# A ViT layer on one core: front's 64-row products widened to 128 rows with zero weights, its square roots taken off ScalarE, a head every 15 slots

## The chip, the cores and the metric

The kernel runs on one core of a Trainium2 chip, in one launch. The metric is the device time of that launch in microseconds (us), the median of three runs.

## The reference

64 images of 112x112 pass through one layer. All is float32; L = 65 tokens (a class token and 8x8), C = 64 channels, H = 8 heads of 8 channels.

```python
h = tok(x)                                 # two-level Haar maps, resized to 8x8, @ W + b: (64, 64, 64)
h = concat([cls_tok, h], axis=1)           # (64, 65, 64)
h = h + attn(layernorm(h))                 # cosine attention
h = h + ffn(layernorm(h))                  # product keys, top 16 of 4096 entries a head, then causal attention

# layernorm: (x - mean) / sqrt(var + 1e-5) over the 64 channels
# attn:      qn = q / max(norm(q), 1e-12), kn likewise, norms over the 8 channels of a head
#            softmax(qn @ kn.T * scale + bias) @ v for each head, then @ proj_w.T + proj_b
```

## The kernel before

**The main stream.** The images go through in ten passes (`PASSES`: 5, 7 seven times, 5, 5, with the two fives at the end; in all 64). A pass has t = 65 times its images as columns: 455 for seven, 325 for five. For each pass and each of the 8 heads the program streams a table of 32 chunks (`CH`) of 128 entries. A chunk is one **slot** `g`; there are 8 x 32 = 256 slots for a pass and 2,560 in all. In slot g TensorE spreads the scores of chunk g + 2 into one of three banks (`spread_scores`, L675, one float32r product of t + 1 columns), ScalarE takes the exponential of chunk g (`exp_unit`, L858), VectorE masks it (`mask_unit`, L1042), and TensorE adds the rows of chunk g - 1 (`add_rows`, L687, a float32 product, which is two instructions). The lead is three banks (`NA`) and four weight buffers (`RING`).

**Beside it.** In the same slots, after those four steps, each engine's program has work in a fixed place, counted modulo 32 (`u`, the chunk of the head): up to four tiles of token scores for the next head, one every 8 slots, with their top-16 search (`scores` L649, `best16` and `top24` on VectorE, `candidates`, `threshold` L443 to L453 and `low_parts` on GpSimd, `turn_scores` L658); and one `attend` for the head before (TensorE at u = 3, 6, 13, 16; VectorE at 4, 5, 9, 10, 17; GpSimd at 6 and 11).

**Front.** While pass p streams, `front` prepares pass p + 1: the maps, the first layernorm, q, k and v, the norms of q and k, eight attention tasks, the projection and the second layernorm. Its place is q, the slot modulo 256:

```python
MAPS, TOK, LN1 = ROWS + 3, ROWS + 6, ROWS + 10          # ROWS = 22, so LN1 = 32
QK, VAL, NRM, ATT = LN1 + 11, LN1 + 14, LN1 + 17, LN1 + 28
PERIOD = 16
```

A task starts at ATT + 16 j; in it TensorE works at steps 0, 8 and 11 (L585, L594, L603), VectorE at 1, 2, 6, 7 and 12, ScalarE at 5 and 9, GpSimd at -2 (`kx`, L412) and 3 (L418). A layernorm takes ten slots from its start (32, and six after the projection): product with `center` (L522), square (L766), copy (L913), one product an image with `mean` (L527), square root (L769), reciprocal (L916), transposes (L532), multiplication (L920). The norms of q and k are one product an image (L570), a square root on ScalarE (L800), a maximum and a reciprocal on VectorE (L936, L940), a spread over the channels on GpSimd (L403) and transposes (L577).

**Order and waits.** The order is written out: every engine loops over the same slots and queues what belongs to each, and then runs its queue strictly in order, waiting for semaphores. Nothing moves past a waiting instruction of its own engine. The front of pass 0 runs in slots -256 to -1, when no chunk streams, with tasks every four slots, beside the folding of the tables (64 groups: `fold`, L625, L822, L634, L991); this stretch is called the prologue here.

## Time and profile before

| | |
|---|---|
| median of three runs | 3162.47 us (3162.01 to 3162.71) |
| the profiled execution | 3162.24 us |
| its span in the trace | 3160.4 us |
| TensorE busy | 3085.8 us, 98% of the span |
| VectorE busy | 2437.1 us, 77% |
| ScalarE busy | 1809.5 us, 57% |
| GpSimd busy | 1102.9 us, 35% |
| prologue, up to the first chunk's spread | 134.6 us |

How to read it: DVE is VectorE, ACT ScalarE, POOL GpSimd, PE TensorE's products and PEld its weight loads, SP SyncE; L687 is line 687 of the kernel before. A matmul's end is modelled, and a group of products also counts as busy while one waits on the next load, so 98% doesn't say that TensorE is at its peak: the starts of successive spreads (L675) show the length of a slot.

### The profile page before, as it was taken

To read this page: it belongs to the slowest core of one execution; us is meant where nothing else is said; L and a number is where in the kernel's file an instruction comes from. 1 tells how busy PE (TensorE), PEld (TensorE's weight loads), DVE (VectorE), ACT (ScalarE), POOL (GpSimd) and SP (SyncE) were. 2 spreads that over 40 slices of the span, in tenths; PEclk is the share of its full clock that TensorE was granted. 3 is DMA by queue.
4 is the path that set the end of the run, shared out by engine and by line. 5 is a ranking of instruction groups with operands and counts; after the bars stand their busy time and mean duration, and the time that the engine had idled before them with its cause. 6 is when DMAs were issued, how large, how long until landed. Compare 5 with 4: busy or idle time off the path is not lost.

```text
span 3160.4 us, 56341 instructions
## 1 busy us (share of the span) xinstructions
PE 3085.8 (98%) x16588; PEld 2020.8 (64%) x16588; DVE 2437.1 (77%) x8690; ACT 1809.5 (57%) x4758; POOL 1102.9 (35%) x2712
## 2 busy tenths in 40 slices
PE   8999999999999999999999999999999999999998
PEld 8867656655666566656666666656655666676666
DVE  4678778877887788777877787778877887787776
ACT  4465565556555655556555655565556565655554
POOL 2234324433443334334433343334333433342331
PEclk9999999999999999999999999999999999999999
DMA  9110000011011101100001000100111001111110
GB/s 222 33 25 18 22 20 19 19 23 20 19 19 23 20 19 19 23 20 14 15 18 26 18 19 19 25 19 19 19 22 20 19 19 21 27 17 26 19 25 18
DMA packets 92763, 81.25 MB, mean 26 GB/s; under 512 B 56542, under 2 KB 87977, under 8 KB 92457
## 3 DMA queue, kind: packets, MB, share of 16 engines
q1 hardware_dynamic: 91505, 77.26, 11.9%
q8 instruction: 135, 2.21, 0.3%
q14 instruction: 171, 1.40, 0.2%
q10 hardware_dynamic: 952, 0.37, 0.1%
HBM read 38.77 MB, written 1.47 MB: 13 GB/s over the span
## 4 chain that ended last, share of the span: by engine, by line
PE 80%; DVE 8%; ACT 5%; issue 4%; POOL 3%; ACTq 0%; DMA 0%; POOLq 0%
PE ps L687 45%; PE ps L675 16%; DVE wts L1042 5%; ACT wts L858 3%; PE ps L716 2%; PE ps L649 2%; PE ps L700 2%; PE ps L603 2%; PE ps L585 2%; PE ps L634 2%; PE ps L658 2%; PE ps L594 1%; PE ps L705 1%; DVE top L1026 1%; PE ps L625 1%
## 5 line engine op out<-in xcount | busy, mean ns | idle before, releaser
L687 PE MATMUL ps<-wts,table 128*128 128x455 f32 (+1 forms) x5120 | 2200.5, 512 | 0.0
L1042 DVE SCALAR_TENSOR_TENSOR wts<-ps,wts 128x455 f32<-128x455 f32 (+1 forms) x2560 | 1473.6, 579 | 537.9 <-ACT wts L858 526.1
L675 PE MATMUL ps<-st,spread 128*128 128x456 f32 (+1 forms) x2560 | 1372.5, 536 | 51.8 <-DVE wts L1042 45.9
L858 ACT ACTIVATE wts<-ps 128x455 f32<-128x455 f32 (+1 forms) x2560 | 1219.3, 513 | 86.5 <-PE ps L675 83.4
L687 PEld LDWEIGHTS ps<-wts,table 128*128 128x128 f32 x5120 | 940.9, 190 | 190.1 <-issue 127.1
L675 PEld LDWEIGHTS ps<-st,spread 128*128 128x128 f32 x2560 | 483.5, 189 | 457.7 <-DVE wts L1042 326.9
L443 POOL TENSOR_SCALAR stat<-top 114x1 f32<-114x1 f32 (+1 forms) x296 | 79.4, 268 | 1317.1 <-DVE top L1026 1317.1
L829 ACT ACTIVATE sc<-ps 114x128 f32<-114x128 f32 (+1 forms) x296 | 82.2, 278 | 349.0 <-PE ps L649 349.0
L833 ACT ACTIVATE cand_e<-top,stat 114x16 f32<-114x16 f32 (+1 forms) x296 | 90.9, 307 | 311.5 <-POOL stat L450 311.2
L848 ACT ACTIVATE st<-ps 128x228 fp32r<-128x228 f32 (+1 forms) x296 | 106.6, 360 | 280.6 <-PE ps L658 280.6
L459 POOL TENSOR_TENSOR parts<-sc,parts 114x128 f32<-114x128 f32 (+1 forms) x296 | 135.3, 457 | 83.3 <-ACT parts L840 74.7
L473 POOL TENSOR_TENSOR s<-s,red 65x455 f32<-65x455 f32 (+1 forms) x80 | 70.6, 882 | 253.0 <-DVE red L1072 253.0
L658 PEld LDWEIGHTS ps<-ident,parts 114*128 114x128 f32 (+1 forms) x592 | 83.8, 142 | 112.2 <-issue 97.2
L1026 DVE MAX8 top<-cand_rest 114x8 f32<-114x100 f32 (+1 forms) x592 | 149.4, 252 | 0.0
L453 POOL TENSOR_SCALAR sc<-sc,stat 114x64 f32<-114x64 f32 (+1 forms) x296 | 138.1, 466 | 29.2
L427 POOL TENSOR_TENSOR cand<-best 114x64 f32<-114x64 f32 (+1 forms) x296 | 87.0, 294 | 135.0 <-DVE best L1010 134.7
L649 PEld LDWEIGHTS ps<-w_sim,xh 128*114 128x114 f32 (+1 forms) x444 | 78.5, 177 | 76.5 <-issue 66.6
L447 POOL TENSOR_SCALAR stat<-stat,top 114x1 f32<-114x1 f32 (+1 forms) x296 | 111.3, 376 | 32.8
L1008 DVE MATCH_REPLACE8 rest<-best,sc 114x64 f32<-114x64 f32 (+1 forms) x592 | 118.2, 205 | 0.0
L412 POOL TENSOR_SCALAR kx<-hx,head_of 64x455 f32<-64x455 f32 (+1 forms) x80 | 107.7, 1346 | 17.8 <-DVE hx L945 17.8
L810 ACT ACTIVATE scratch<-ps 65x455 f32<-65x455 f32 (+1 forms) x80 | 41.1, 514 | 118.2 <-PE ps L594 118.2
L658 PE MATMUL ps<-ident,parts 114*128 114x114 f32 (+1 forms) x592 | 106.4, 260 | 0.0
(141 smaller groups left out, 3449.8 us busy)
## 6 DMA issues: line engine op xcount, KB each, us to landing
st<-st SPq DMA_DIRECT2D x320, 114.0 KB, 3.8
table<-in_table SPq DMA_DIRECT2D x128, 128.0 KB, 5.2
rz_row<-rz_dram SPq DMA_DIRECT2D x56, 228.0 KB, 4.2
rz_row<-rz_dram SPq DMA_DIRECT2D x24, 165.0 KB, 4.2
scratch<-in_x SPq DMA_DIRECT2D x7, 343.0 KB, 4.1
rz_dram<-rz SPq DMA_DIRECT2D x56, 1.8 KB
out<-s SPq DMA_DIRECT2D x7, 113.8 KB
scratch<-in_x SPq DMA_DIRECT2D x3, 245.0 KB, 3.6
```

Source lines behind the costliest of these rows:

```text
L412: P.tensor_scalar(kx[0:C, j % 2, 0:t], xf[:, 0:t], head_of[0:C, j:j + 1], None, ALU.mult)\
L447: P.tensor_scalar(sn[:, 0:1], sn[:, 0:1], sn[:, 1:2], tp[:, 0:1], ALU.min, ALU.add)\
L453: P.tensor_scalar(sc[0:tt, n % SCR, 0:NK], sc[0:tt, n % SCR, 0:NK], sn[:, 1:2], None, ALU.add)\
L459: P.tensor_tensor(parts[0:tt, n % 2, :, 1, :].rearrange("p (k s) m -> p k s m", s=2), sc[0:tt, n % SCR, :].rearrange("p (s k m) -> p k s m ...
L649: mm(ps[0:tt, TK, 0:128], src[:, t * tt:(t + 1) * tt], w_sim[:, k % H, :], start=True, stop=True).then_inc(sc_mm, 1)
L658: last = tr(ps[0:128, TK, x * tt:(x + 1) * tt], parts[0:tt, n % 2, 2 * x:2 * x + 2, :, :].rearrange("p k l m -> p (k l m)"), ident[0:tt, 0 ...
L675: mm(ps[0:128, g % NA, 0:t], spread[:, q * 128:(q + 1) * 128], st[:, k % 2, ORDER[c // QUADS], 0:t], start=True, stop=True).then_inc(a_rea ...
L687: mm(ps[0:128, ACC + k % 2, 0:t], table[:, k % H, i, :], wts[:, g % RING, 0:t], start=(c == 0), stop=(c == CH - 1)).then_inc(out_done, 1)
L858: A(wts[:, g % RING, 0:t], ps[0:128, g % NA, 0:t], ACT.Exp).then_inc(e_ready, 1)
L1008: V.match_replace(rest[0:tt, side, :], top8, s, LOWEST).then_inc(best_ready, 1)
L1026: V.max(top[0:tt, n % SCR, 8 * i:8 * i + 8], src).then_inc(top_ready, 1)
L1042: V.scalar_tensor_tensor(out=wts[:, g % RING, 0:t], in0=ps[0:128, g % NA, 0:t], scalar=0.0, in1=wts[:, g % RING, 0:t], op0=ALU.is_ge, op1= ...
```

## The change

Three things change. **(1)** The products of `front` that contracted 64 rows now contract 128: `center`, `mean`, `w_qk`, `w_v` and `w_proj` become 128 rows high, with zeros in the half that isn't wanted, and read all of `hx` (or `sq`) in place of its half. `center` and `w_proj` also become 128 columns wide, again with zeros. **(2)** ScalarE takes no square root. In a layernorm it adds epsilon, and GpSimd raises the result to -0.5 (L413 of the new file), in place of VectorE's reciprocal. For the norms of q and k VectorE takes the maximum with 1e-24, makes a start value by a shift and a subtraction on the bits, and does three Newton steps of three instructions each; each of the eleven instructions has a slot of its own and waits for the one before. **(3)** The tasks start nine slots later (ATT = LN1 + 37 = 69) and follow each other every 15 slots, so that the eighth starts at 174 in place of 172, and the second layernorm at 194 in place of 192. `nrm`, its two companions and `bias_row` move into `scratch`.

```diff
+NRM_STEPS = 2 + 3 * 3
+RSQRT_START = 1597463007.0
...
-QK, VAL, NRM, ATT = LN1 + 11, LN1 + 14, LN1 + 17, LN1 + 28
-PERIOD = 16
+QK, VAL, NRM, ATT = LN1 + 11, LN1 + 14, LN1 + 17, LN1 + 37
+PERIOD = 15
...
-        v_center = sb("v_center", [128, C])
-        w_v, center = v_center[0:C, :], v_center[C:128, :]
+        w_v, center = sb("w_v", [128, C]), sb("center", [128, 128])
         head_of = sb("head_of", [128, 2 * H])
-        w_qk, b_qk = sb("w_qk", [C, 128]), sb("b_qk", [128, 1])
-        b_v, w_proj = sb("b_v", [L, C]), sb("w_proj", [C, C])
+        w_qk, b_qk = sb("w_qk", [128, 128]), sb("b_qk", [128, 1])
+        b_v, w_proj = sb("b_v", [L, C]), sb("w_proj", [128, 128])
         q_scale = sb("q_scale", [C, 1])
...
-        eps, mean = sb("eps", [128, 1]), sb("mean", [C, 1])
+        eps, mean = sb("eps", [128, 1]), sb("mean", [128, 1])
+        power = sb("power", [L, NMAX])
...
+        nrm_y, nrm_t = scratch[0:L, 1000:1112], scratch[0:L, 1120:1232]
         kx = sb("kx", [128, 2, TP])
-        nrm, o_tok = sb("nrm", [L, NMAX * 2 * H]), sb("o_tok", [L, NMAX, C])
+        nrm, o_tok = scratch[0:L, 1240:1352], sb("o_tok", [L, NMAX, C])
+        bias_row = scratch[0:H, 1360:1360 + 2 * L - 1]
...
+            P.memset(power[:, :], -0.5).then_inc(set_pool, 1)
...
+            P.memset(center[0:C, :], 0.0).then_inc(set_pool, 1)
+            P.memset(w_proj[0:C, 0:C], 0.0).then_inc(set_pool, 1)
...
+            P.memset(center[C:128, C:128], 0.0).then_inc(set_pool, 1)
+            P.memset(w_proj[C:128, :], 0.0).then_inc(set_pool, 1)
+            P.memset(w_qk[C:128, :], 0.0).then_inc(set_pool, 1)
+            P.memset(w_v[C:128, :], 0.0).then_inc(set_pool, 1)
...
+            def layernorm(p, q, n, start):
+                i = 2 * p + n
+                if q == start + 6:
+                    pool.wait_ge(std_ready, i + 1)
+                    P.tensor_tensor(std[:, 0:PASSES[p]], std[:, 0:PASSES[p]], power[:, 0:PASSES[p]], ALU.pow)\
+                        .then_inc(inv_ready, 1)
...
+                layernorm(p, q, 0, LN1)
+                layernorm(p, q, 1, after_tasks(p) + 6)
+                if q == NRM + 13:
+
+                    pool.wait_ge(nrm_inv, NRM_STEPS * (p + 1))
                     P.tensor_copy(inv[:, 0:n, :].rearrange("p b (h d) -> p b h d", d=HD),
-                                  by_image(nrm[:, 0:n * 2 * H], n).unsqueeze(3).to_broadcast([L, n, 2 * H, HD]))\
+                                  by_image(nrm_y[:, 0:n * 2 * H], n).unsqueeze(3).to_broadcast([L, n, 2 * H, HD]))\
...
-                    mm(ps[0:C, FR, 0:t], center, hf[:, 0:t], start=True, stop=True).then_inc(cen_mm, 1)
+                    mm(ps[0:128, FR, 0:t], center[:, :], hx[:, 0:t], start=True, stop=True).then_inc(cen_mm, 1)
...
-                        last = mm(ps[0:L, FR, b:b + 1], of_image(sq[0:C, :], b), mean[:, :], start=True, stop=True)
+                        last = mm(ps[0:L, FR, b:b + 1], of_image(sq, b), mean[:, :], start=True, stop=True)
...
-                    mm(ps[0:128, FR, 0:t], w_qk[:, :], xf[:, 0:t], start=True, stop=True).then_inc(qk_mm, 1)
+                    mm(ps[0:128, FR, 0:t], w_qk[:, :], hx[:, 0:t], start=True, stop=True).then_inc(qk_mm, 1)
...
-                        last = mm(ps[0:L, FR, b * C:(b + 1) * C], of_image(xf, b), w_v, start=True, stop=True)
+                        last = mm(ps[0:L, FR, b * C:(b + 1) * C], of_image(hx, b), w_v[:, :], start=True, stop=True)
...
-                if q == NRM + 6:
+                if q == NRM + 15:
...
-                    mm(ps[C:128, FR, 0:t], w_proj[:, :], xf[:, 0:t], start=True, stop=True).then_inc(proj_mm, 1)
+                    mm(ps[0:128, FR, 0:t], w_proj[:, :], hx[:, 0:t], start=True, stop=True).then_inc(proj_mm, 1)
...
-                    A(sq[0:C, 0:t], ps[0:C, FR, 0:t], ACT.Square).then_inc(sq_ready, 1)
+                    A(sq[:, 0:t], ps[0:128, FR, 0:t], ACT.Square).then_inc(sq_ready, 1)
...
-                    A(std[:, 0:PASSES[p]], ps[0:L, FR, 0:PASSES[p]], ACT.Sqrt, bias=eps[0:L, 0:1])\
+                    A(std[:, 0:PASSES[p]], ps[0:L, FR, 0:PASSES[p]], ACT.Identity, bias=eps[0:L, 0:1])\
...
-                if q == NRM + 1:
-                    act.wait_ge(nrm_mm, p + 1)
-                    A(nrm[:, 0:n * 2 * H], ps[0:L, FR, 0:n * 2 * H], ACT.Sqrt).then_inc(nrm_ready, 1)
...
-                if q == start + 6:
-                    dve.wait_ge(std_ready, i + 1)
-                    V.reciprocal(std[:, 0:PASSES[p]], std[:, 0:PASSES[p]]).then_inc(inv_ready, 1)
...
-                if q == NRM + 2:
-                    dve.wait_ge(nrm_ready, p + 1)
-                    V.tensor_scalar(nrm[:, 0:n * 2 * H], nrm[:, 0:n * 2 * H], 1e-12, None, ALU.max)\
+                if q == NRM + 1:
+                    dve.wait_ge(nrm_mm, p + 1)
+                    V.tensor_scalar(nrm[:, 0:n * 2 * H], ps[0:L, FR, 0:n * 2 * H], 1e-24, None, ALU.max)\
                         .then_inc(nrm_max, 1)
-                if q == NRM + 3:
-                    dve.wait_ge(nrm_max, p + 1)
-                    V.reciprocal(nrm[:, 0:n * 2 * H], nrm[:, 0:n * 2 * H]).then_inc(nrm_inv, 1)
-                if q == NRM + 7:
+                if 0 <= q - NRM - 2 < NRM_STEPS:
+
+                    step = q - NRM - 2
+                    x, y, t = nrm[:, 0:n * 2 * H], nrm_y[:, 0:n * 2 * H], nrm_t[:, 0:n * 2 * H]
+                    if step == 0:
+                        dve.wait_ge(nrm_max, p + 1)
+                        V.tensor_scalar(t.bitcast(I32), x.bitcast(I32), 1, None, ALU.logical_shift_right)\
+                            .then_inc(nrm_inv, 1)
+                    else:
+                        dve.wait_ge(nrm_inv, NRM_STEPS * p + step)
+                    if step == 1:
+                        V.tensor_scalar(y.bitcast(I32), t.bitcast(I32), -1.0, RSQRT_START, ALU.mult, ALU.add)\
+                            .then_inc(nrm_inv, 1)
+                    if step >= 2 and step % 3 == 2:
+                        V.tensor_tensor(t, y, y, ALU.mult).then_inc(nrm_inv, 1)
+                    if step >= 2 and step % 3 == 0:
+                        V.scalar_tensor_tensor(out=t, in0=t, scalar=-0.5, in1=x, op0=ALU.mult, op1=ALU.mult)\
+                            .then_inc(nrm_inv, 1)
+                    if step >= 2 and step % 3 == 1:
+                        V.scalar_tensor_tensor(out=y, in0=t, scalar=1.5, in1=y, op0=ALU.add, op1=ALU.mult)\
+                            .then_inc(nrm_inv, 1)
+                if q == NRM + 16:
```

Three places in the order of the instructions. The first is **ScalarE's queue while the first pass streams, about slot 50**, where the norms of q and k are taken (L858 and, in the new file, L875 are the exponential of a chunk; L829/L846 and L848/L865 copy scores of the tiles). Before:

```order
L829 ACTIVATE sc<-ps 110x128
L858 ACTIVATE wts<-ps 128x325
L800 ACT_TABLE_LOAD
L800 ACTIVATE nrm<-ps 65x112
L858 ACT_TABLE_LOAD
L858 ACTIVATE wts<-ps 128x325
L848 ACTIVATE st<-ps 128x2x110
L858 ACTIVATE wts<-ps 128x325 x6
```

Now:

```order
L846 ACTIVATE sc<-ps 110x128
L875 ACTIVATE wts<-ps 128x325 x2
L865 ACTIVATE st<-ps 128x2x110
L875 ACTIVATE wts<-ps 128x325 x6
```

The square root and a table load on either side of it are gone; the whole program keeps one table load, its first.

The second is **VectorE's queue at the same slots** (L1042 and L1074 are the mask of a chunk; L1006/L1038 and L1010/L1042 are searches of the tiles, so that L1042 means another thing in the new file). Before:

```order
L1042 SCALAR_TENSOR_TENSOR wts<-ps,wts 128x325
L1008 MATCH_REPLACE rest<-best,sc 110x64 x2
L936 TENSOR_SCALAR nrm<-nrm 65x112
L1042 SCALAR_TENSOR_TENSOR wts<-ps,wts 128x325
L940 RECIPROCAL nrm<-nrm 65x112
L1042 SCALAR_TENSOR_TENSOR wts<-ps,wts 128x325
```

Now:

```order
L1038 MAX best<-sc 110x8 x2
L950 TENSOR_SCALAR scratch<-ps 65x112
L1074 SCALAR_TENSOR_TENSOR wts<-ps,wts 128x325
L1040 MATCH_REPLACE rest<-best,sc 110x64 x2
L958 TENSOR_SCALAR scratch<-scratch 65x112
L1074 SCALAR_TENSOR_TENSOR wts<-ps,wts 128x325
L963 TENSOR_SCALAR scratch<-scratch 65x112
L1074 SCALAR_TENSOR_TENSOR wts<-ps,wts 128x325
L1042 MAX best<-rest 110x8 x2
L966 TENSOR_TENSOR scratch<-scratch 65x112
L1074 SCALAR_TENSOR_TENSOR wts<-ps,wts 128x325
```

Where a reciprocal stood between two masks, a chain begins that puts one instruction of 65x112 behind each of twelve masks.

The third is **GpSimd's queue while the first pass streams**, where a task's `kx` stands against the five instructions of `threshold` (L443 to L453 before, L463 to L473 now; L427/L430 and L447/L450 are the candidates). Before, the sixth task's `kx`, in slot 138 (u = 10):

```order
L412 TENSOR_SCALAR kx<-hx,head_of 64x455
L473 TENSOR_TENSOR s<-s,red 65x325
L443 TENSOR_SCALAR stat<-top 110x1
L444 TENSOR_SCALAR stat<-stat,top 110x1
L447 TENSOR_SCALAR stat<-stat,top 110x1
```

Now, the seventh task's `kx`, in slot 157 (u = 29):

```order
L464 TENSOR_SCALAR stat<-stat,top 110x1
L467 TENSOR_SCALAR stat<-stat,top 110x1
L470 TENSOR_SCALAR stat<-stat,top 110x1
L473 TENSOR_SCALAR sc<-sc,stat 110x64
L432 TENSOR_SCALAR kx<-hx,head_of 64x455
L447 TENSOR_TENSOR cand<-best 110x64
```

At a period of 16 every `kx` stood ahead of the threshold of its tile; at 15 the place moves by one slot a task, and this one stands behind it.

## Rows read from the trace of the kernel before

**Rows 1.** The page, parts 1 and 2: busy us of each engine, TensorE's clock

```profile
PE 3085.8 (98%) x16588; PEld 2020.8 (64%) x16588; DVE 2437.1 (77%) x8690; ACT 1809.5 (57%) x4758; POOL 1102.9 (35%) x2712
...
PEclk9999999999999999999999999999999999999999
```

**Rows 2.** The page, part 4: the chain that ended last, by engine

```profile
PE 80%; DVE 8%; ACT 5%; issue 4%; POOL 3%; ACTq 0%; DMA 0%; POOLq 0%
```

**Rows 3.** Six stretches: us, then busy us of each engine (x instructions)

```profile
688.28:725.05 36.77, 36.54 (x155) 21.84 (x155) 29.39 (x107) 20.97 (x56) 12.32 (x34) 1.00 0.14 29
486.49:526.80 40.31, 40.31 (x227) 26.20 (x225) 33.19 (x117) 22.82 (x60) 17.02 (x39) 1.00 0.11 19
465.10:477.48 12.38, 11.54 (x66) 6.89 (x64) 8.54 (x30) 8.00 (x17) 3.29 (x9) 1.00 0.00 0
707.17:716.55 9.38, 9.34 (x43) 5.70 (x43) 7.21 (x27) 4.92 (x14) 2.63 (x8) 1.00 0.00 0
646.65:668.08 21.43, 21.24 (x109) 12.93 (x108) 17.29 (x59) 13.67 (x31) 6.58 (x18) 1.00 0.13 31
685.78:704.85 19.07, 19.02 (x87) 11.39 (x85) 16.06 (x57) 10.80 (x28) 7.46 (x20) 1.00 0.27 56
```

**Rows 4.** Groups by line: line engine op names shapes xcount | busy us, mean ns

```profile
L858 ACT ACT_TABLE_LOAD x27 | 34.6, 1283 | 0.5
...
L769 ACT ACT_TABLE_LOAD x20 | 25.7, 1283 | 0.4
...
L800 ACT ACT_TABLE_LOAD x9 | 11.5, 1283 | 0.2
...
L940 DVE RECIPROCAL nrm<-nrm 65x112 f32<-65x112 f32 (+1 forms) x10 | 7.7, 773 | 0.0
...
L522 PEld LDWEIGHTS ps<-hx,v_center 64*64 64x64 f32 x40 | 3.8, 131 | 2.6
```

**Rows 5.** The chain about slot 50: start us, us, what

```profile
469.73 1.01 ACT L858
...
471.61 0.63 DVE wts L1042
...
474.98 0.48 PE ps L675
```

**Rows 6.** Timeline of PE: start us, us, engine line

```profile
446.35 0.92 PE L687 MATMUL ps<-wts,table 128*128 128x455 f32 x2
447.12 0.99 PE L700 MATMUL ps<-kv,xh 128*65 128x65 f32 x14
447.91 0.45 PE L675 MATMUL ps<-st,spread 128*128 128x456 f32 x1
448.20 0.93 PE L687 MATMUL ps<-wts,table 128*128 128x455 f32 x2
449.06 0.98 PE L527 MATMUL ps<-mean,scratch 64*65 64x1 f32 x14
449.97 0.48 PE L675 MATMUL ps<-st,spread 128*128 128x456 f32 x1
```

**Rows 7.** POOL: one line's instructions, ns min/median/max, and one row of its timeline

```profile
L412 POOL TENSOR_SCALAR kx<-hx,head_of x80: 1097/1446/1454, 50.8 to 2835.8; 64x455 f32<-64x455 f32 x56, 64x325 f32<-64x325 f32 x24
...
450.20 0.47 POOL L453 TENSOR_SCALAR sc<-sc,stat 114x64 f32<-114x64 f32 x1
```

**Rows 8.** Timeline of PEld in the place of rows 6

```profile
447.12 0.85 PEld L700 LDWEIGHTS ps<-kv,xh 128*65 128x65 f32 x13 [0.24 <-issue]
...
449.05 0.90 PEld L527 LDWEIGHTS ps<-mean,scratch 64*65 64x65 f32 x14 [0.66 <-issue]
```

**Rows 9.** One stretch, u = 2 to 6, beside a task's step 6

```profile
489.41:495.47 6.06, 6.06 (x37) 3.71 (x35) 5.91 (x22) 3.48 (x10) 2.04 (x7) 1.00 0.01 3
```

**Rows 10.** The chain at the end of the prologue's front: start us, us, what

```profile
98.60 0.69 PE ps L522 x2
...
104.51 0.49 DVE hx L920
```

More of the change, by code:

```diff
@@ L23 @@
 F32R = mybir.dt.float32r
+I32 = mybir.dt.int32
 ALU = mybir.AluOpType
@@ L175, in build @@
         qk_mm, qk_out, qk_sq, v_mm, v_out = sem("qk_mm"), sem("qk_out"), sem("qk_sq"), sem("v_mm"), sem("v_out")
-        nrm_mm, nrm_ready, nrm_max, nrm_inv = sem("nrm_mm"), sem("nrm_ready"), sem("nrm_max"), sem("nrm_inv")
+        nrm_mm, nrm_max, nrm_inv = sem("nrm_mm"), sem("nrm_max"), sem("nrm_inv")
         nrm_spread, nrm_turned, qk_unit = sem("nrm_spread"), sem("nrm_turned"), sem("qk_unit")
@@ L234, in build @@
         bias_dram = nc.dram_tensor("bias_dram", (L * (BIAS_PITCH + 1),), F32, kind="Internal").ap()
-        bias_row = sb("bias_row", [H, 2 * L - 1])
         s2, pt2 = sb("s2", [L, NMAX * L + 1]), sb("pt2", [L, TP])
@@ L288, in build @@
                      (w_tok[:, :, :].rearrange("p j c -> p (j c)"), "w_tok"), (tok_b, "tok_b"),
-                     (cls_tok, "cls_tok"), (center, "center")]
-        consts_act = [(rel, "rel"), (mlp1, "mlp1"), (pk_q, "pk_q"), (pk_k, "pk_k"), (w_qk[:, :], "w_qk"),
-                      (b_qk[:, :], "b_qk"), (w_v, "w_v"), (b_v[:, :], "b_v"), (head_of[:, :], "head_of"),
-                      (q_scale[:, :], "q_scale"), (w_proj[:, :], "w_proj"), (b_proj, "b_proj"),
+                     (cls_tok, "cls_tok"), (center[C:128, 0:C], "center")]
+        consts_act = [(rel, "rel"), (mlp1, "mlp1"), (pk_q, "pk_q"), (pk_k, "pk_k"), (w_qk[0:C, :], "w_qk"),
+                      (b_qk[:, :], "b_qk"), (w_v[0:C, :], "w_v"), (b_v[:, :], "b_v"), (head_of[:, :], "head_of"),
+                      (q_scale[:, :], "q_scale"), (w_proj[0:C, C:128], "w_proj"), (b_proj, "b_proj"),
                       (causal[:, :], "causal")]
@@ L510, in _ @@
             pe.wait_ge(set_act, 5)
-            pe.wait_ge(set_pool, 10)
+            pe.wait_ge(set_pool, 17)
             def layernorm(p, q, n, start):
@@ L906, in _ @@
             dve.wait_ge(set_act, 5)
-            dve.wait_ge(set_pool, 10)
+            dve.wait_ge(set_pool, 17)
             def layernorm(p, q, n, start):
```

8 lines of the change are left out of this document (3 added, 5 removed).

## The prediction

> **What bounds the kernel now.** I read the page first. TensorE is busy 98% of the span at the full clock, VectorE 77%, the rest far less [rows 1]; the chain that ended last lies on TensorE for 80% and on VectorE, ScalarE and GpSimd for 16% together [rows 2]. So it is TensorE's stream, with places where a mask or an exponential comes late, and what the change is worth must be read slot by slot. The stretches say where [rows 3]. 32 slots of seven images without front take 36.77 us; the same 32 with two tasks take 40.31, for 72 more products: 3.54 / 72 = 49 ns each. That is about what a small product costs TensorE, so added or removed TensorE time counts in full in both. VectorE is busy for 29.39 and 33.19 us of them, 80 and 82%: room on average, not everywhere.
>
> There are nine fronts beside a streaming pass and one in the prologue; I count by nine, and the last apart.
>
> **The square roots.** ScalarE loads a table before each root and again before the next exponential: 27 + 20 + 9 loads by these lines and a few in the prologue, of 1283 ns [rows 4]. All but the program's first go. ScalarE is not the bound, so what they cost is what TensorE waits for:
> - Norms of q and k: eight slots with the root take 12.38 us, the same eight without front 9.38 [rows 3]. 23 more products account for 23 x 0.049 = 1.13; 1.87 us is left. The chain shows it: the load, the exponential behind it, the mask, and only then the spread at 474.98 [rows 5].
> - Layernorm: the 16 slots of the second one take 21.43 us against 19.07 [rows 3], 2.36 more. The `center` product takes 0.77 (a 455-column float32 pair, from the start at 446.35 to that of the next group at 447.12 [rows 6]), its 21 small ones 1.03; 0.56 is left, of which 0.42 is the next part's. So a root there costs 0.14, since the load runs while ScalarE would wait for the variance anyway.
>
> Sum: 1.87 + 2 x 0.14 = 2.15 us a front, 9 x 2.15 = **-19.4**. Ends: -11 if a third of the norms' stall comes back as waits for its neighbours and the layernorms give nothing (9 x 1.25); -35 if a load of 1.28 us for each root was on the chain (3 x 9 x 1.28).
>
> The mask at 471.61 begins 1.88 us after the load at 469.73 [rows 5]; the load's 1.28 leaves 0.6 for the exponential and nothing else. The Trainium skill (ScalarE: Activation LUTs, What ACT_TABLE_LOAD costs) gives 1283 ns and a drain of 1380 ns, 2.66 us for a switch. The duration agrees; the drain has no room in the trace, and were it real and exposed at the norms, the term would be -19.4 - 9 x 2 x 1.38 = -44, an estimate from that page. I keep the trace's.
>
> **What takes their place.** VectorE gets twelve instructions of 65x112 for two and loses two small reciprocals. The largest of those it loses takes 773 ns [rows 4]; I put a new one at 0.2, so 12 x 0.2 - 1.3 = +1.1 us a front. In its eight slots VectorE idles 12.38 - 8.54 us with the stall and 9.38 - 7.21 without [rows 3], one instruction a slot: hidden, **0**. With that cover gone it would be 9 x 1.1 = +10. GpSimd gets two powers of 65x7. No row has a power there; the nearest are a 114x64 scalar operation, 0.47, and the 64x455 `kx`, 1.45 [rows 7]. I take the near one, 0.4 us. TensorE wants it two slots later, some 2.5 us: hidden, **0**; at 1.45, and behind `attend`'s subtraction in the first layernorm, it would be late by up to 0.7, +6 over nine fronts.
>
> **The widened products.** Two groups of 14 products, loads of 65 columns both, follow a pair of L687. The one with 128 rows has its next spread 447.91 - 446.35 = 1.56 us after the pair's start, the one with 64 rows 449.97 - 448.20 = 1.77 [rows 6]: 0.21 more, though it moves one column in place of 65. The first weight load of the 64-row group waits 0.66 us for no engine, the other's later load 0.24 [rows 8]: it doesn't overlap the product before. Seven groups of a front are widened (`center` and `mean` twice, `w_qk`, `w_v`, `w_proj`): 7 x 0.21 = 1.47 us, 9 x 1.47 = **-13.2**. Upper end 7 x 0.42 x 9 = -26 by the load's wait. Other end: nothing gained, and two loads of three products twice as wide, at 131 ns [rows 4] 6 x 0.13 = 0.8 a front, +7. `attend`'s 64-row transposes (L705) stay.
>
> The row says 64 rows cost 0.21 us more at the switch. The Trainium skill (TensorE: Matmul & The Clock Gate, LDWEIGHTS) states that a load's time depends on its columns and not its rows, which speaks against the change: nothing for `mean`, `w_qk` and `w_v`, and a loss for the other two. For the load itself nothing contradicts it; the difference lies before it.
>
> **Tasks every 15 slots.** The same work in other places. At 16, tasks began at u = 28 and 12 alone. At 15 they begin at u = 5, 20, 3, 18, 1, 16, 31, 14. Two things follow.
> - VectorE is full at u = 2 to 6 where a task's step 6 falls there: 5.91 of 6.06 us [rows 9]. Before, every second task put one reduction there. Now the third and fifth put their steps 1 and 2 in it, the seventh its steps 1, 2 and 6 at u = 0, 1 and 5. They bring TensorE work of their own, so only part shows: I take 0.4 us a front.
> - GpSimd: two `kx`, for u = 31 and 16, are now queued behind the threshold of a tile. From there it is the last 0.47 us step, candidates, and 1.45 for `kx` [rows 7], for a product two or three slots on; queued behind that product are the row additions on TensorE. I take 0.3 us each.
>
> 1.0 us a front, **+9**. Ends: 0 (the banks absorb it), +27 (each of the two `kx` late by a slot, 1.2 us, and 0.6 for VectorE).
>
> **Prologue.** The second layernorm of the first front ran beside the folding, from 98.60 to 104.51 + 0.49 [rows 10], 6.4 us. Now it starts at slot 117, when the early folds are issued; up to 6.4 us show, less its TensorE part, and six table loads beside the folds go. **+2**, between -3 and +6. The extra fills on GpSimd lie in the wait for the constants.
>
> **Sum.** 3162.24 (the profiled execution, 0.2 below the median; 1.8 of it lie outside the span) - 19.4 - 13.2 + 9 + 2 = 3140.6. What a measurement of this kernel can tell from no change is 0.2%, 6.3 us.
>
> **The rivals.**
> - *The new period costs nothing*, the root is worth more than I read off: -19.4 to -35 with -13.2 and +2, so 3116 to 3132. For: three banks of lead, and 7.1 us of idle VectorE in the 32 slots with tasks [rows 3]. Against: the full stretch [rows 9]. Chance 0.25.
> - *The period takes most of it back*: +27 in place of +9, 3159 at the worst; 3148 to 3156 for the middle of it. Chance 0.12.
> - *Widening gives nothing* and the wait in [rows 8] is only shown elsewhere: 3140.6 + 13.2 = 3154, or up to 3161 with the wider loads. The Trainium skill's rule on loads (same page) would be this case. The switch measured in [rows 6] speaks against. Chance 0.08.
> - *No change*: two of these together, or table loads that only fill time in which a mask waits for something else. 3156 to 3169. Chance 0.07.
> - *Slower, by GpSimd's power.* It sits in a strict queue between the candidates and the low parts of a tile, and TensorE's transposes wait for it, with all row additions behind them. Its margin is about 1.5 us; each us more costs 18 us over 18 layernorms. From 1.5 + 28 / 18 = 3.1 us for a power the time passes 3169. Seven elements a partition speak against, nothing shows the operation. Chance 0.06: 3169 to 3190.
>
> **The numbers.** My forecast, 3134 to 3148, has 0.42. Faster by over 0.2% are that, the free period, the costly period and the idle widening: 0.87; within 0.2%: 0.07; slower: 0.06. The range 3118 to 3156 leaves out the last two cases, the worst of the costly period and of the idle widening, and the best 2 us of the free period.
>
> **What would show it.** Right: one table load left; the eight slots of the norms at some 10.5 us; the wait of 0.66 gone before L547 (the new `mean`) and the group at 1.56; powers under 0.5 us; the 128 slots with tasks a little dearer per task than 1.77 us. Wrong: a group of `mean` still at 1.77; masks waiting for ScalarE at slot 50; TensorE waiting for `kx` by more than 0.5 us or for the power at all; total waits of spreads for masks larger than before.

## The result, and the profile after

The changed kernel takes **3169.1 us** (median of 16 runs, 3168.14 to 3171.21), the kernel before 3162.49 in the same comparison (16 runs, 3161.27 to 3163.31). The ratio is 1.0022, with a 95% interval from 1.0014 to 1.0029: slower by 6.6 us. I had forecast 3140.6, and my range ended at 3156. The profiled execution took 3169.04 us, 1.8 of them outside its span.

The page, first the busy times, then the chain that ended last by engine (its span is 3167.2 us):

```profile
PE 3079.0 (97%) x16588; PEld 2027.7 (64%) x16588; DVE 2441.1 (77%) x8770; ACT 1741.4 (55%) x4690; POOL 1130.6 (36%) x2739
...
PE 72%; DVE 12%; issue 5%; ACT 5%; POOL 5%; ACTq 0%; DMA 0%; POOLq 0%; DVEq 0%
```

Against [rows 1, 2]: TensorE's share of the chain has fallen from 80% to 72%, and VectorE, ScalarE and GpSimd hold 22% where they held 16. Busy time hardly moved; what grew is the share of the chain that runs over the other engines. By place in the span, of the 6.8 us between the two profiled executions 6.1 lie before the first spread and 0.7 behind it: over the nine fronts beside a streaming pass gains and losses nearly cancel.

**How the slots were priced.** Every slot begins with a spread, so the starts of successive spreads give each slot's length. A pass has 256 slots. Of the 32 values of u, I took for each the length of a slot in which no front work runs (in all kernels here 36.7 us for the 32) and call what a slot takes above this its *extra*. The table is the median over five seven-image passes, us per pass; its last line is read once, from each profiled execution. "After" is the changed kernel, the other columns are experiments below:

```
                                   before    e1    e13   after    e2     e3     e4    e12
first layernorm, slots 33 to 43      3.34   3.34   2.88   2.54   2.88   3.11   2.54   2.53
w_qk and w_v, slots 44 to 49         1.72   1.72   1.05   1.05   1.04   1.72   1.05   1.05
norms, to the first task             3.19   3.18   3.16   2.64   3.17   2.42   2.41   2.50
the eight tasks                     14.74  18.23  18.15  18.21  14.63  15.27  15.28  14.82
behind them (second layernorm)       3.78   5.95   5.27   3.01   2.95   3.58   2.65   2.65
whole pass, us                     324.67 330.34 328.28 325.13 322.72 323.76 321.57 321.21
first spread starts at, us          134.6  139.3  136.5  140.7  132.8  136.6  134.6  134.8
```

Read column "after" against "before": everything has become cheaper but the tasks, 3.5 us dearer for the same eight heads, and the prologue, 6.1 us longer. Passes with five images differ: the first, which prepares seven, goes from 264.3 to 265.9 us, the last three are 1 to 1.4 us shorter each. The stretches of the two kernels, with the same slots in each. The first row is a whole pass, the second the eight slots of the norms, the third the slots of the eight tasks (128 at a period of 16, 120 at 15), the fourth the 22 slots behind them; they are cut within 0.3 us of the spreads. Columns are those of [rows 3]. Of the kernel before:

```profile
722.54:1047.22 324.68, 322.16 (x1652) 200.96 (x1650) 257.15 (x905) 188.75 (x481) 118.66 (x290) 1.00 0.10 20
789.87:802.25 12.38, 11.54 (x66) 6.89 (x64) 8.54 (x30) 7.99 (x17) 3.29 (x9) 1.00 0.01 2
805.80:967.39 161.59, 161.59 (x906) 105.27 (x904) 133.19 (x467) 91.44 (x237) 66.61 (x151) 1.00 0.10 19
967.39:997.23 29.84, 29.52 (x147) 17.38 (x144) 22.38 (x78) 18.97 (x46) 9.72 (x26) 1.00 0.11 24
```

And of the changed kernel:

```profile
730.41:1055.50 325.09, 321.70 (x1650) 201.51 (x1650) 257.61 (x913) 181.86 (x474) 121.60 (x292) 1.00 0.11 20
796.16:806.92 10.76, 10.72 (x58) 6.64 (x57) 8.22 (x32) 4.87 (x13) 2.62 (x8) 1.00 0.01 2
821.88:977.18 155.30, 153.78 (x861) 98.99 (x859) 124.74 (x438) 86.24 (x221) 63.83 (x143) 1.00 0.09 15
977.18:1006.23 29.05, 28.99 (x151) 18.13 (x151) 22.06 (x73) 16.61 (x44) 11.17 (x27) 1.00 0.08 25
```

In its task slots before, TensorE was busy without a gap: 161.59 of 161.59 us. After, it stands still for 155.30 - 153.78 = 1.52 us, less than half of the 3.5 that the tasks became dearer; the rest doesn't show as idle time. (128 quiet slots take 4 x 36.7 = 146.8 us, so the tasks cost 14.8. The 120 quiet slots at the same values of u take 137.1, and the tasks 18.2.) The norms' eight slots do what I forecast, 10.76 us for the 10.5.

The widened `mean` and its neighbours. First the TensorE timeline about the group that answers to L527, then its first weight load:

```profile
455.62 0.93 PE L707 MATMUL ps<-wts,table 128*128 128x455 f32 x2
456.38 0.94 PE L547 MATMUL ps<-mean,scratch 128*65 128x1 f32 x14
457.18 0.45 PE L695 MATMUL ps<-st,spread 128*128 128x456 f32 x1
...
456.00 0.14 PEld L547 LDWEIGHTS ps<-mean,scratch 128*65 128x65 f32 x1 [0.19 <-issue]
```

From the pair's start at 455.62 to the next spread at 457.18 are 1.56 us, where the 64-row group had 1.77 [rows 6], and the wait of 0.66 us before its first load [rows 8] is 0.19. A single wide product, `w_qk`, before and after:

```profile
782.76 0.93 PE L687 MATMUL ps<-wts,table 128*128 128x455 f32 x2
783.62 1.03 PE L559 MATMUL ps<-hx,w_qk 64*128 64x455 f32 x2
784.58 0.47 PE L675 MATMUL ps<-st,spread 128*128 128x456 f32 x1
784.89 0.54 PE L687 MATMUL ps<-wts,table 128*128 128x455 f32 x1
```

```profile
790.00 0.93 PE L707 MATMUL ps<-wts,table 128*128 128x455 f32 x2
790.77 0.93 PE L579 MATMUL ps<-hx,w_qk 128*128 128x455 f32 x2
791.18 0.72 PE L695 MATMUL ps<-st,spread 128*128 128x456 f32 x1
791.74 0.54 PE L707 MATMUL ps<-wts,table 128*128 128x455 f32 x1
```

To the next spread it is 1.18 us for 1.82, but the next pair of row additions follows that spread later, so from pair to pair it is 1.74 for 2.13: 0.39 saved.

GpSimd's power (its line's instructions: minimum, median and maximum in ns, then the first and the last start):

```profile
L413 POOL TENSOR_TENSOR std<-std,power x20: 1192/1510/1516, 36.7 to 2875.6; 65x7 f32<-65x7 f32 x14, 65x5 f32<-65x5 f32 x6
```

And two groups by line, the one table load that is left and one of the new instructions on VectorE:

```profile
L768 ACT ACT_TABLE_LOAD x1 | 1.3, 1283 | 8.0 <-issue 8.0
L966 DVE TENSOR_TENSOR scratch<-scratch 65x112 f32<-65x112 f32 (+1 forms) x30 | 7.4, 245 | 0.0
```

The power takes 1.2 us for 65x5 and 1.51 us for 65x7, where I took 0.4.

### The profile page after: what moved, and what is told of

It reads as the page before. It is cut to its first block, busy times and chain, and to the rows that moved or that the text cites. A ratio compares the mean times of both kernels' runs of the same rounds, so it can differ in the third digit from the quotient of the medians.

```text
span 3167.2 us, 56380 instructions
## 1 busy us (share of the span) xinstructions
PE 3079.0 (97%) x16588; PEld 2027.7 (64%) x16588; DVE 2441.1 (77%) x8770; ACT 1741.4 (55%) x4690; POOL 1130.6 (36%) x2739
## 3 DMA queue, kind: packets, MB, share of 16 engines
q8 instruction: 135, 2.21, 0.3%
## 4 chain that ended last, share of the span: by engine, by line
PE 72%; DVE 12%; issue 5%; ACT 5%; POOL 5%; ACTq 0%; DMA 0%; POOLq 0%; DVEq 0%
PE ps L707 40%; PE ps L695 14%; DVE wts L1074 6%; ACT wts L875 3%; PE ps L736 2%; PE ps L605 2%; PE ps L720 2%; PE ps L623 2%; PE ps L669 2%; PE ps L654 2%; PE ps L678 1%; DVE top L1058 1%; PE ps L725 1%; POOL stat L467 1%; DVE cand_rest L1060 1%
## 5 line engine op out<-in xcount | busy, mean ns | idle before, releaser
L1074 DVE SCALAR_TENSOR_TENSOR wts<-ps,wts 128x455 f32<-128x455 f32 (+1 forms) x2560 | 1475.5, 579 | 551.0 <-ACT wts L875 538.4
L695 PE MATMUL ps<-st,spread 128*128 128x456 f32 (+1 forms) x2560 | 1387.7, 542 | 57.2 <-DVE wts L1074 49.5
L875 ACT ACTIVATE wts<-ps 128x455 f32<-128x455 f32 (+1 forms) x2560 | 1228.0, 512 | 171.2 <-PE ps L695 167.2
L463 POOL TENSOR_SCALAR stat<-top 114x1 f32<-114x1 f32 (+1 forms) x296 | 78.5, 265 | 1165.4 <-DVE top L1058 1163.8
L865 ACT ACTIVATE st<-ps 128x228 fp32r<-128x228 f32 (+1 forms) x296 | 106.3, 359 | 318.2 <-PE ps L678 318.2
L846 ACT ACTIVATE sc<-ps 114x128 f32<-114x128 f32 (+1 forms) x296 | 82.0, 277 | 301.3 <-PE ps L669 301.1
L1058 DVE MAX8 top<-cand_rest 114x8 f32<-114x100 f32 (+1 forms) x592 | 149.4, 252 | 0.0
L473 POOL TENSOR_SCALAR sc<-sc,stat 114x64 f32<-114x64 f32 (+1 forms) x296 | 137.3, 464 | 29.1
L438 POOL TENSOR_TENSOR scratch<-scratch,red 65x455 f32<-65x455 f32 (+1 forms) x80 | 70.2, 878 | 157.8 <-DVE red L990 157.8
L447 POOL TENSOR_TENSOR cand<-best 114x64 f32<-114x64 f32 (+1 forms) x296 | 85.2, 288 | 108.2 <-DVE best L1042 108.2
L1040 DVE MATCH_REPLACE8 rest<-best,sc 114x64 f32<-114x64 f32 (+1 forms) x592 | 118.2, 205 | 0.0
```

The costliest lines, as they stand in the source:

```text
L473: P.tensor_scalar(sc[0:tt, n % SCR, 0:NK], sc[0:tt, n % SCR, 0:NK], sn[:, 1:2], None, ALU.add)\
L695: mm(ps[0:128, g % NA, 0:t], spread[:, q * 128:(q + 1) * 128], st[:, k % 2, ORDER[c // QUADS], 0:t], start=True, stop=True).then_inc(a_rea ...
L875: A(wts[:, g % RING, 0:t], ps[0:128, g % NA, 0:t], ACT.Exp).then_inc(e_ready, 1)
L1040: V.match_replace(rest[0:tt, side, :], top8, s, LOWEST).then_inc(best_ready, 1)
L1058: V.max(top[0:tt, n % SCR, 8 * i:8 * i + 8], src).then_inc(top_ready, 1)
L1074: V.scalar_tensor_tensor(out=wts[:, g % RING, 0:t], in0=ps[0:128, g % NA, 0:t], scalar=0.0, in1=wts[:, g % RING, 0:t], op0=ALU.is_ge, op1= ...
```

## The experiments

All times are medians; each ratio is to the kernel before, timed in the same series, with its 95% interval. I first took the change apart: its three parts alone, and the two that should pay together.

**e1: the new places alone.** The kernel before with

```diff
-QK, VAL, NRM, ATT = LN1 + 11, LN1 + 14, LN1 + 17, LN1 + 28
-PERIOD = 16
+QK, VAL, NRM, ATT = LN1 + 11, LN1 + 14, LN1 + 17, LN1 + 37
+PERIOD = 15
```

> The kernel before with the new task places alone (ATT = LN1 + 37, period 15); its roots and its 64-row products stay. Theory A, the period takes back what the rest gains: the eight tasks of a front cost 18.2 us over the quiet slots in the changed kernel against 14.8 before, so 3.4 us for each of nine fronts, 31 us, and up to 6 us in the prologue: 3190 to 3199 us. Theory B, the period costs the 1 us a front that was forecast and the loss comes from what replaces the roots (eleven more instructions on VectorE, the powers on GpSimd) or from the widened products: 3171 to 3177 us.

Measured: 3215.26 us against 3160.93, 1.0174 (1.0158 to 1.0189), **+54.3**, above both ranges: I had priced what the tasks and the prologue showed, and not the second layernorm. The whole loss of the change is here, and far more than it. Two rows of the trace of e1 (the eight tasks; the 22 slots behind them) say where in a pass:

```profile
834.50:989.91 155.41, 153.87 (x856) 98.79 (x855) 124.29 (x436) 86.96 (x222) 64.08 (x143) 1.00 0.08 15
989.91:1021.93 32.02, 29.96 (x152) 17.47 (x151) 22.50 (x75) 19.12 (x46) 9.76 (x26) 1.00 0.10 23
```

The task slots take what those of the changed kernel take, 155.41 and 155.30. Behind them TensorE idles 32.02 - 29.96 = 2.06 us where it idled 29.84 - 29.52 = 0.32 before: here the second layernorm's root on ScalarE, worth only 0.2 at its old place (e3), holds up the masks. In the chain through these slots the exponential's table load, the exponential and the mask stand in a row:

```profile
1007.72 1.28 ACT L858
1009.02 0.56 ACT wts L858
...
1010.65 0.49 DVE wts L1042
```

**e2: the widening alone**, everything else as before (its edits are those of the diff on `center`, `mean`, `w_qk`, `w_v`, `w_proj` and the squares).

> The kernel before with the five products of front widened to 128 rows, nothing else. If the 0.21 us at each switch to 64 rows is TensorE's own time: 9 x 1.47 = 13 us less, 3147 to 3151 us, and the first weight load of each widened group waits 0.2 us and not 0.66. If the wait only shows elsewhere, or the 128-column loads cost something: 3160 to 3170 us. Theory A wants the first.

Measured: 3143.3 us, 0.9944 (0.9929 to 0.9959), **-17.6**, more than the 13.2 of my term and below my range. This decides between the trace's rows and the page: the Trainium skill (TensorE: Matmul & The Clock Gate, LDWEIGHTS) has a load's time depend on its columns and not its rows. For the load itself the traces agree, 136 ns for 64 rows of 65 columns and 139 for 128 rows; but by that alone this edit saves nothing, and it saves 0.56%. The gain lies in the time between the products.

**e3: the roots alone.** The changed kernel with 64-row products, tasks at their old places and, so that the norms end before them, three of VectorE's dependent instructions in a slot:

```diff
-                if q == NRM + 13:
+                if q == NRM + 6:
...
-                if 0 <= q - NRM - 2 < NRM_STEPS:
-
-                    step = q - NRM - 2
+                for step in range(NRM_STEPS):
+                    if q != NRM + 2 + step // 3:
+                        continue
```

> The kernel before without ScalarE's square roots: the power on GpSimd, and the Newton chain with three instructions in a slot in place of one, so that it takes four slots and the tasks stay where they were (60, period 16). 64-row products stay. Theory A: the stall of 1.87 us at the norms and 0.14 at each layernorm go, 9 x 2.15 = 19 us, less at most 1.1 us a front for the additional VectorE work: 3143 to 3154 us. Theory B: what replaces the roots costs about as much as they did, or more: 3160 us or above.

Measured: 3155.73 us, 0.9983 (0.9973 to 0.9993), **-5.2**, outside both ranges, and not the 19 that the roots should give by my term.

**e4: both, at the old places**: e3 with the widened products.

> The changed kernel with the Newton chain in four slots and the tasks back at 60 with period 16: roots off ScalarE and widened products together, without the new places. Theory A: the two gains add, 3130 to 3141 us, faster than both kernels. Theory B: 3155 us or above.

Measured: 3136.71 us, 0.9924 (0.9909 to 0.9938), **-24.2**, as expected: the two parts add up (17.6 + 5.2 = 22.8). It is the changed kernel but for the places and for three steps of the chain in a slot, and 32 us faster.

**e13: new places and widening, roots left on ScalarE**, to see what the roots are worth there.

> The changed kernel with its square roots back on ScalarE and the reciprocals on VectorE: widened products and new places, nothing else. Slot by slot the root's absence gives 1.65 us at the norms and 0.26 at each layernorm, 2.2 us a front, in the old places of the second layernorm; in the new ones (start 194) the run with the places alone showed 2.2 us more a front behind the tasks. Theory A: both go with the roots, (2.2 + 2.2) x 9 = 40 us at most, less 1 to 2 us for the power in the prologue; so this kernel is 25 to 38 us slower than the changed one, 3194 to 3207 us. Theory B, the chain and the powers cost much of what the roots did: within 15 us of the changed kernel, below 3185 us.

Measured: 3197.41 us against 3160.84, 1.0117 (1.01 to 1.0134), **+36.6**. So at the new places widening gives 54.3 - 36.6 = 17.7, as at the old ones, and taking the roots off gives 36.6 - 6.6 = 30.0 (26 between the two profiled executions, 3195.28 and 3169.04). Widening is additive. The roots are not: they repair part of what the new places break (the second layernorm: 5.27 against 3.01 in the table, and 3.16 against 2.64 at the norms). In the prologue taking them off costs instead: the first spread starts 4.2 us later than in e13.

**Is it the period or the places?** I had said that at 15 the tasks come upon full slots. e6 and e7 are e4, period 16, with the tasks at two other pairs of places:

```diff
-QK, VAL, NRM, ATT = LN1 + 11, LN1 + 14, LN1 + 17, LN1 + 28
+QK, VAL, NRM, ATT = LN1 + 11, LN1 + 14, LN1 + 17, LN1 + 31
```

for e6 (u = 31 and 15), and `LN1 + 35` for e7 (u = 3 and 19).

> The version with both gains and period 16 (3136.7 us), its tasks moved from slot 60 to 63, so that they start at u = 31 and 15. Theory P, what counts is the place modulo 32 and not the period: in the changed kernel the tasks at u = 31 and 16 cost 1.73 and 2.00 us over the quiet slots, against 1.98 and 1.62 at u = 28 and 12, so about 0.1 us a task more or less: 3130 to 3146 us. Theory Q, it is the period of 15 itself, the tasks being closer together: no change, within 3 us of 3137.

> The same with the tasks at 67, period 16: u = 3 and 19. Theory P: tasks at u = 3 cost 2.54 us in the changed kernel, at 18 and 20 2.21, so (2.54 + 2.2) / 2 - 1.80 = 0.57 us more for each of 72 tasks, 41 us: 3165 to 3190 us (2 to 6 us of it from the prologue, where the second layernorm comes later). Theory Q: 3137 to 3144 us.

Measured: e6 3160.45 against 3162.91, 0.9991 (0.9982 to 1.0001); e7 3165.98, 1.0009 (0.9999 to 1.0018). Against e4, at the old period, three slots of delay cost 21 to 24 us and seven 27 to 29 (by the ratios, by the medians). For e6 neither theory had it: I had expected 3130 to 3146. Price of one task by its place, extra us:

```
period 16   u=28 1.98   u=12 1.61  (before)    u=31 1.93  u=15 1.69  (e6)    u=3 2.52  u=19 1.68  (e7)
period 15   u=5 2.68  u=20 2.21  u=3 2.54  u=18 2.21  u=1 2.46  u=16 2.00  u=31 1.73  u=14 2.37  (after)
```

(Medians of the tasks at a place. At period 16 the last task, and in e3, e4 and e6 also the first, costs 0.4 to 0.8 more; the table above has that in it.) A task at u = 3 costs 2.5 us at either period. It is the place. The two tasks that I had priced for GpSimd, u = 31 and 16, are the cheapest of the eight in a seven-image pass. But e6's tasks cost 16.0 a pass and its seven-image passes stay 1.9 us below those of before (322.79); what it loses against e4 is for the larger part in the first, five-image pass, 271.65 us against 263.31, in the last full one of that size, 257.3 against 253.0, and in the prologue, 137.3 against 134.6. In the first pass a task at u = 31 costs 3.1 us, against 1.3 at u = 28 in the kernel before. The slots are shorter there and `kx`, prepared for seven images, takes as long as ever. The changed kernel has one such task, its seventh, 2.8 us, whose `kx` is the one shown behind the threshold. GpSimd's rows, then TensorE's:

```profile
311.18 0.46 POOL L473 TENSOR_SCALAR sc<-sc,stat 110x64 f32<-110x64 f32 x1
311.63 1.45 POOL L432 TENSOR_SCALAR kx<-hx,head_of 64x455 f32<-64x455 f32 x1
...
313.13 1.04 PE L605 MATMUL ps<-kx,qk 128*65 128x65 f32 x14 [1.01 <-POOL kx L432]
```

From spread to spread this slot takes 2.97 us. Over the whole of e6 TensorE waits so 23 times:

```profile
PE ps L605 <- POOL kx L432: 17.3, 23, 1.5
```

**What the places cost: VectorE.** The chain of waits of the changed kernel through the task at u = 5 (start, us, engine, tile, line), its middle:

```profile
826.16 0.57 PE ps L725 x7
...
827.19 0.54 ACT wts L875
...
828.72 0.58 DVE wts L1074
829.29 0.23 DVE cand_rest L1060
...
831.85 0.39 DVE rest L1040 x2
832.24 0.53 DVE red L997
832.77 0.54 DVE wts L1074
...
837.58 0.47 PE ps L695
```

Between 826.73 and 837.58 no row of this chain is one of TensorE's: the masks (L1074) stand behind the tiles' searches (L1058, L1060, L1040) and behind the task's own sum (L997), and the spread waits for the mask. (In its last 4 us it also runs over a threshold on GpSimd and ScalarE's copies.) Before, the chains of all eight tasks lay on TensorE entirely. e10 shortens only the task's part of that work: both of its reductions in the changed kernel run over two columns of 65. The diff shows the sum; the maximum is cut likewise, and the exponential is taken of a hundredth of the scores, so the attention's weights are not the layer's.

```diff
-                    V.tensor_reduce(red[:, j % 2, 1, 0:n], by_image(expo[:, j % 2, 0:t], n), AX.X, ALU.add)\
+                    V.tensor_reduce(red[:, j % 2, 1, 0:n], by_image(expo[:, j % 2, 0:t], n)[:, :, 0:2], AX.X, ALU.add)\
```

> The changed kernel with VectorE's two reductions of a task (the row maximum and the row sum) over 2 columns of an image in place of 65, and the exponential of a hundredth of the scores, so the attention's weights are others: the instructions and waits stay, about 1 us of VectorE's time a task goes. GpSimd's subtraction stays. Theory V, at u = 1, 3 and 5 a task's reductions fall on VectorE's full slots: these three tasks, now 2.46 to 2.68 us, fall to 1.6 to 2.0, the one at 18 keeps its 0.5 us of GpSimd, in all 1.5 to 2.5 us a front: 3146 to 3156 us. Theory W, it is ScalarE's and TensorE's strict order at these places (copies and groups of the attend in the same slots): 3165 to 3169 us.

> The same edit in the version with both gains, tasks at 60, period 16 (3136.7 us). Its tasks run at TensorE's pace, so under both theories little is gained: 3130 to 3137 us. If it gains as much as in the changed kernel, VectorE's time counts everywhere and not by place.

Measured: e10 3147.54 against 3161.99, 0.9955 (0.994 to 0.997), **21.6 us** below the changed kernel; e11, the same edit in e4, 3134.93, 0.9913 (0.9897 to 0.993), 2 to 4 below e4. The one edit is worth 21.6 at the new places and next to nothing at the old ones. A task's two reductions shrink from 610 and 609 ns to 152 and 151, as e10's instructions of one of them show:

```profile
L990 DVE TENSOR_REDUCE red<-scratch x80: 141/151/158, 60.5 to 2832.5; 65x7 f32<-65x14 f32 x56, 65x5 f32<-65x10 f32 x24
```

Its task slots take 153.10 us in place of 155.30:

```profile
815.92:969.02 153.10, 152.71 (x858) 99.06 (x857) 117.92 (x438) 86.27 (x222) 63.77 (x143) 1.00 0.08 15
```

TensorE's idle time there is 0.39 us, from 1.52. By place, in seven-image passes, the price falls at u = 5 (2.68 to 2.22), 3 (2.54 to 2.08), 20 (2.21 to 1.76), 18 (2.21 to 1.79), 14 (2.37 to 2.11) and 16 (2.00 to 1.85); it does not move at u = 1 and 31 (2.46 to 2.45, 1.73 to 1.73). I had expected u = 1 to fall with 3 and 5, and all three further, to 1.6 to 2.0. The chain through the task at u = 1 lies on TensorE entirely, like those of before. The task's own groups are 0.84 us of L605, 0.41 of L614 and 0.78 of L623 there, 2.03 together. At the old places a task cost less than that, 1.98 and 1.61; at u = 1 all of it and 0.4 more. So VectorE is some 2.2 of the 3.5 us and GpSimd some of the rest (below). The remainder I put down to TensorE's own products meeting no slack; that was read from the chain and from a price that no edit moved, not undone by an edit, and isn't shown.

**What the places cost: GpSimd.** The chain through the task at u = 18:

```profile
884.32 0.84 PE ps L605 x14
...
888.26 0.46 POOL sc L473
888.72 0.92 POOL scratch L438
...
890.15 0.54 ACT wts L875
...
892.78 0.47 PE ps L695
```

GpSimd's subtraction (L438, 0.92 us) waits behind a tile's threshold (up to L473), and the exponential behind it. e8 leaves the subtraction out of the changed kernel and lets ScalarE wait for the maxima themselves, again with the exponential of a hundredth of the scores; e9 does the same in e4.

> The changed kernel without GpSimd's subtraction of the row maximum in the tasks; ScalarE waits for VectorE's maximum and takes the exponential of a hundredth of the scores, so the attention's weights are others. If the cost of the new places lies in GpSimd's queue, the subtraction standing behind a tile's threshold and ScalarE's exponential of a chunk behind the task's: the task at u = 18 loses 0.4 to 0.6 us, others 0.1 to 0.3, in all 1 to 2 us a front, 3151 to 3160 us. If it lies with VectorE's full slots and the chunk's mask behind them: 3166 to 3169 us, since VectorE's work is unchanged.

> The same subtraction left out of the version with both gains and period 16. The chain of its tasks lies wholly on TensorE, so nothing is gained there: 3133 to 3137 us. If it gains as much as the same edit does in the changed kernel, GpSimd's queue has nothing to do with the places.

Measured: e8 3165.01 against 3162.91, 1.0006 (0.9996 to 1.0015), 4 to 5 us below the changed kernel and between my two ranges; e9 3139.44, 0.9925 (0.991 to 0.994), not below e4's 0.9924, so nothing is gained there (my range, 3133 to 3137, was missed by 2 us, and the kernel before took 2 us more in this series than in e4's). In the trace of e8 one place changes clearly, u = 18, from 2.21 to 1.65; the eight tasks together cost 17.5 for 18.2, and the first spread starts 1.9 us earlier. So beside the `kx` of the five-image pass another GpSimd instruction at another place costs 0.5 us a front.

**e12: a version that beats both.** If the places must stay, the norms have to start earlier in place of ending later. `NRM` and `VAL` change places, so that the chain runs under the value product, with two instructions a slot. Against e4 (the waits and the steps behind the chain move with it):

```diff
-QK, VAL, NRM, ATT = LN1 + 11, LN1 + 14, LN1 + 17, LN1 + 28
+QK, NRM, VAL, ATT = LN1 + 11, LN1 + 14, LN1 + 17, LN1 + 28
...
-                    if q != NRM + 2 + step // 3:
+                    if q != NRM + 2 + step // 2:
```

> A version that keeps the tasks at 60 with period 16 and makes room for the Newton chain by taking the norms' products before v's (slots 46 and 49 exchanged), two instructions of the chain in a slot. In the changed kernel's trace the slots with one chain instruction each cost nothing over the quiet slots; with three a slot they cost about 1.5 us a front. If two a slot are nearly free: 3136.7 - 9 x 1.2 = 3124 to 3130 us. If two cost as three do: 3134 to 3138 us.

Measured: 3132.07 against 3161.99, 0.9905 (0.989 to 0.992), **-29.9**, the fastest kernel of the study. Its task slots on a pass, to be held against the row of before:

```profile
798.23:959.78 161.55, 161.55 (x902) 105.15 (x901) 133.69 (x469) 91.07 (x236) 67.36 (x152) 1.00 0.11 19
```

TensorE doesn't stop in them, and they cost what they cost before. The time lies between my two ranges: two dependent instructions a slot are not free (2.50 at the norms in the table); the changed kernel's one a slot add nothing in eight of the slots 53 to 61 (extra 0.00) and 0.26 in the ninth.

## Why the prediction was wrong

**The term that failed is "Tasks every 15 slots", +9 with an upper end of +27.** Alone it measures +54.3 (e1), where I had tasks a little dearer and nothing else. Three things were wrong in it.
- *Its base.* I charged 0.4 for VectorE and 0.6 for GpSimd to the tasks that meet full slots, and nothing to the rest. But the old places, u = 28 and 12, were not neutral: with 14.74 us for eight tasks, 1.84 each, they were better than seven of the eight new ones in a seven-image pass. At u = 12 a task cost less than its products take end to end. My 49 ns per small product was an average over exactly those slots, and I took it for a price that holds anywhere. The tasks became dearer by 3.5 a front where I had 1.0.
- *What else moves.* `ATT` and the period also move the second layernorm: at its new place ScalarE's root makes it 2.2 us dearer (e1, 5.95 against 3.78). And in the changed kernel the chain pushes the norms' transposes and the unit step to slots 64 and 65; slots 62 to 69 have an extra of 1.2 a front, of which the transposes' own share, about 0.4, only changed place. I had priced neither.
- *The cause named for more than half of it.* The two `kx` (u = 31 and 16), 0.6 of my 1.0 us, cost nothing that shows in a seven-image pass: those tasks are the cheapest. The mechanism is real where the slots are shorter: in the first pass TensorE waits 1.0 us for `kx` at u = 31, which I had named as a sign of being wrong. Beside it GpSimd's queue cost at u = 18, through the subtraction (e8). VectorE's part was the right cause, sized at 0.4 and measured at 2.2 (e10).

Was the upper end wrong by the size or by the way it was built? By the way: I bounded the waits by one slot and never by all that tasks can cost. The trace of before could have warned: two tasks cost 3.54 us there [rows 3], less than twice the 2.03 of a task's groups laid end to end, so the old places were good ones, and a move had more to lose than to gain.

**The roots, -19.4: right at the place, wrong as a sum.** The norms' stall is gone as forecast. Over slots 50 to 59 the extra falls from 3.4 to 1.4 us, of which I put some 0.4 down to transposes that moved elsewhere: 1.65 for my 1.87. Each layernorm gives 0.2 to 0.3 for my 0.14. Together some 2.2 a front for my 2.15, counting only these slots. What I had put at nothing was not nothing: the chain that takes their place is nearly free only when one instruction goes to a slot, and this is why the tasks had to wait, the 54 us of e1. At the old places, three a slot, the roots are worth 5 to 7 us (e3; e4 less e2); with two a slot and an earlier start 12 (e12 less e2). One cause in the forecast, that VectorE idles in these eight slots, was true and beside the point: to cost next to nothing, eleven dependent steps need eleven slots.

**GpSimd's power, 0 and hidden: size wrong, verdict nearly right.** It took 1.51 us, not 0.4. That is the margin of 1.5 that I gave it, and so TensorE's products wait for it in only 3 of the 20 layernorms. Two rows of the waits of the changed kernel's TensorE over the whole span, us in total, times and the longest, the second for `kx`:

```profile
PE ps L552 <- POOL std L413: 2.9, 3, 1.6
PE ps L605 <- POOL kx L432: 1.9, 2, 1.0
```

**The widened products, -13.2: right in kind, too small.** Measured 17.6 and 17.7. The groups of 14 gave 0.21 to 0.26, as I had it. But the four single products of 455 columns gave 0.34 to 0.40 each from pair to pair (`w_qk` above; to the next spread alone it looks like 0.6). Four of these and three groups come to 2.2 a front; the passes got shorter by 1.95. I had multiplied all seven by the price of a group of small ones.

**The prologue, +2 between -3 and +6: at its upper end.** It measures 140.7 - 134.6 = 6.1, nearly all that the changed kernel lost. I had counted the roots' going as a gain here. But the first spread starts 2.0 us later without them at the old places (e3) and 4.2 later at the new ones (after against e13; part of it is the clock, see below). The second layernorm now shows, as I wrote it might, and the chain of waits has it, with the power in it:

```profile
102.86 0.69 DVE table L1023
...
107.36 1.20 POOL std L413
...
110.04 0.73 PE ps L669 x2
```

**Sum.** By the runs: +54.3 for the places, -17.7 for widening there, -30.0 for the roots there, in all +6.6. Of the 30.0 much only undoes what the places had brought. Slot by slot, a seven-image pass has -0.8 at the first layernorm, -0.7 at `w_qk` and `w_v`, -0.55 at the norms, +3.5 at the tasks, -0.8 behind them and some -0.2 in quiet slots: +0.46. With the passes of other sizes nine fronts come to +0.7, and the prologue to 6.1. **On the rivals**: I gave 0.12 to the costly period and put its worst at 3159. That mechanism happened, and alone it is twice as dear as its worst. The measured time lies at the edge of two others, "no change" and "slower, by GpSimd's power". That is chance: the first wanted two rivals together or idle table loads, where one rival alone did it, and the power would have needed 3.1 us.

## What to carry to other kernels

The same small products cost from 1.6 to 2.7 us a task here by the slot they fall in, and in a pass with shorter slots the order of the places was another. So price a move by what the work costs at the new place without any slack (here the 2.03 us of its groups end to end), and take the difference, not by the average price of such work at the old one; and ask what else the move takes along. And when a change buys a stall with a delay (here an eleven-step chain, one step a slot), ask first whether the chain can start earlier in place of ending later: e12 took the gain of both and left the tasks alone. Rows of zeros that make a 64-row product 128 rows high were a gain by themselves here, where the products around it have 128, at both sets of places.
